# Relation types in the slots of the gathered rows, eight blocks of rows held, and the last four node blocks as two groups of two

## The reference

```
x = x + GRU(red, h)    h = layernorm(x), red[n] = sum over edges to n of h[src] + relvectors[type]
x = x + FFN0(layernorm(x))       shared MLP and 4 experts, top 2
x = x + out / (deg + 1)          out[n] = sum over edges to n of (layernorm(x) @ W.T + b)[src]
x = x + FFN1(layernorm(x))       8 experts of 256 x 1024 x 256, top 2
```

## Time and profile before

| | us |
|---|---|
| median of 3 runs | 3529.81 (3520.11 to 3531.26) |
| the profiled execution | 3538.93 |
| its span | 3537.4 |
| PE busy | 2454.6 (69%) |
| POOL busy | 1839.2 (52%) |
| DVE busy | 1507.1 (43%) |
| ACT busy | 767.8 (22%) |

### The profile page before, as it was taken

How to read it: one execution, slowest core, us unless ns; L and a number is a source line. 1 busy time by engine, 2 the same in 40 slices (tenths; PEclk the granted TensorE clock), 3 DMA queues, 4 the chain that set the end, 5 groups by cost and what they waited for, 6 DMA issues and landing times. The chain is left out here.

```text
span 3537.4 us, 56704 instructions
## 1 busy us (share of the span) xinstructions
PE 2454.6 (69%) x14176; PEld 1894.3 (54%) x14177; DVE 1507.1 (43%) x3886; ACT 767.8 (22%) x1370; POOL 1839.2 (52%) x2044
## 2 busy tenths in 40 slices
PE   1288888888877666546577766654444799999991
PEld 1265555555555453324355544333222699999991
DVE  5544444444453342313466454442311544555545
ACT  1222222222222111002111100000000345444450
POOL 0243334444555566770777777777775344444440
PEclk7578788788777776557677776666555899999996
DMA  5321122122222223330433333333332222211116
GB/s 136 97 62 50 52 59 71 58 69 70 82 76 79 82 83 95 102 101 9 116 109 109 102 113 107 107 107 101 110 104 83 80 66 67 67 58 62 54 44 227
DMA packets 157788, 302.92 MB, mean 86 GB/s; under 512 B 47333, under 2 KB 91784, under 8 KB 157720
## 3 DMA queue, kind: packets, MB, share of 16 engines
q0 software_dynamic: 85984, 234.74, 22.9%
q1 hardware_dynamic: 40876, 36.11, 3.4%
q10 hardware_dynamic: 30860, 31.40, 2.7%
HBM read 261.73 MB, written 40.39 MB: 85 GB/s over the span
## 5 line engine op out<-in xcount | busy, mean ns | idle before, releaser
L733 POOL DMA_INDIRECT rows<-table,srcT x1568 | 1536.5, 980 | 942.8 <-issue 465.7
L793 PE MATMUL bank<-rows,onehot 128*128 x3904 | 794.2, 349 | 673.7 <-POOLq L726 553.7
L793 PEld LDWEIGHTS bank<-rows,onehot 128*128 x3904 | 417.8, 113 | 908.6 <-issue 780.2
L759 DVE SCALAR_TENSOR_TENSOR onehot<-iota_row,tbase,dstT 128x512 f16 x488 | 367.2, 754 | 639.5 <-PE bank L793 225.9
L1733 PE MATMUL bank<-xe_high,W_high 128*128 128x256 f32 x864 | 252.7, 292 | 30.2 <-DVE xe_low L1811 30.0
L1783 ACT ACTIVATE hid<-bank,b 128x256 f32<-128x256 f32 x432 | 181.8, 472 | 346.6 <-PE bank L1735 346.4
L1734 PE MATMUL bank<-xe_low,W_high 128*128 128x256 f32 x864 | 250.7, 290 | 0.0
L1735 PE MATMUL bank<-xe_high,W_low 128*128 128x256 f32 x864 | 250.3, 290 | 0.0
L1819 DVE TENSOR_TENSOR hid_low<-hid,hid_high 128x512 fp32r<-128x512 f32 x216 | 149.7, 693 | 235.9 <-ACT hid_high L1787 235.9
L1733 PE MATMUL bank<-W_high,hid_high 128*128 128x256 f32 x864 | 248.3, 287 | 0.0
L1735 PE MATMUL bank<-W_high,hid_low 128*128 128x256 f32 x864 | 243.8, 282 | 0.0
(11 more groups left out here) (340 smaller groups left out, 3744.1 us busy)
## 6 DMA issues: line engine op xcount, KB each, us to landing
rows<-table,srcT POOLq DMA_INDIRECT x1568, 2.8
W<-in_L_ffn_W_dram SPq DMA_DIRECT2D x14, 1024.0 KB, 7.4
y<-results ACTq DMA_DIRECT2D x12, 1024.0 KB, 10.0
x_res<-in_x_dram SPq DMA_DIRECT2D x1, 6144.0 KB, 44.1
table<-part ACTq DMA_DIRECT2D x12, 512.0 KB, 3.2
normal<-xn ACTq DMA_DIRECT2D x12, 512.0 KB, 3.4
out_dram<-x_res SPq DMA_DIRECT2D x12, 512.0 KB
table<-part SPq DMA_DIRECT2D x6, 512.0 KB, 2.9
```

The source lines that it names most:

```text
L733: nc.gpsimd.indirect_dma_start(out=rows[:, k % (M * U), :], out_offset=None, in_=q.table, in_offset=bass.IndirectOffsetOnAxis(srcT[:, k:k ...
L759: last = nc.vector.scalar_tensor_tensor(onehot[:, ds(slot, U), :], iota_row[:, :].unsqueeze(1).to_broadcast([P, U, P]), base, dstT[:, ds(k ...
L793: last = nc.tensor.matmul(sums, hot, ring_rows[:, ds(row0 + (s * PARTS + part_) * D, D)], start=False, stop=False, skip_group_check=True)
```

## The change

- The ring `rows` of layer 0 has a pitch of 544 numbers: 512 gathered ones and two slots of 16 for types. DVE writes the type one-hot of a chunk into the first slot (columns 512 to 527) if this is the block's first use, else into the second, which nothing reads. `typehot` goes; the second matmul of a chunk takes 272 columns, low half and types together, and the third one goes. `typeT` becomes f16.
- `M` = 8: both layers' rings of rows hold eight blocks instead of four. The landing semaphores stay four (`LANDED`). `PASS` is rounded up to a multiple of 8 (208 in place of 200).
- The groups are 1, eleven of 4, and two of 2 tiles (`SIZES`). For the last two, which stand unrolled behind the loop, a window follows steps 0 and 2 only. So step 3 of the second last group follows W48, and only two tiles' steps follow that.
- `ctT` lies in `work[0:16, 0, :]`.

```diff
@@ -33,17 +33,22 @@
 GROUPS = NT // GW
+SIZES = [1] + [GW] * (GROUPS - 1) + [GW // 2] * 2
+LAST = len(SIZES) - 1
 W = GW * P
...
 U = 4
-M = 4
+M = 8
 MH = 8
+LANDED = 4
 BLOCKS = CHUNKS // U
-PASS = BLOCKS + M
+PASS = -(-(BLOCKS + M) // M) * M
 SPAN = 1024
...
 PARTS = 2
+ROW = PARTS * D
+PITCH = ROW + 2 * RELS
 SCALE = 2048.0
@@ -64,7 +69,7 @@
 def program(nc, a, out):
-    assert NT == GROUPS * GW + 1 and EP * EJ * P >= NE and BLOCKS % M == 0 and PASS % M == 0
+    assert NT == GROUPS * GW + 1 and EP * EJ * P >= NE and BLOCKS % LANDED == 0 and M == MH and PASS % M == 0
@@ -109,7 +114,7 @@
         dstT = sb("dstT", [P, KCOLS], F32, graph)
-        typeT = sb("typeT", [P, KCOLS], F32, graph)
+        typeT = sb("typeT", [P, KCOLS], F16, graph)
         srcT = sb("srcT", [P, CHUNKS], I32, graph)
@@ -162,16 +167,20 @@
+        def size(g):
+            return SIZES[g] if isinstance(g, int) else GW
         def first_tile(g):
-            return NT - 1 - g * GW if isinstance(g, int) else g * -GW + (NT - 1)
+            return NT - first_window(g) - size(g) if isinstance(g, int) else g * -GW + (NT - 1)
...
-            return 0 if isinstance(g, int) and g == 0 else GW - 1 - i
+            return size(g) - 1 - i
         def first_window(g):
-            return 0 if isinstance(g, int) and g == 0 else g * GW - (GW - 1)
+            return sum(SIZES[:g]) if isinstance(g, int) else g * GW - (GW - 1)
@@ -216,13 +225,12 @@
-            return (sb(f"rows{n}", [P, M * U, PARTS * D], F16, where),
+            return (sb(f"rows{n}", [P, M * U, (PITCH, ROW)[n]], F16, where),
                     sb(f"onehot{n}", [P, MH * U, P], F16, where), sb(f"spare{n}", [P, 1], F32, where),
...
         rows, onehot, spare, stats, mean_var, stdev, rstd = layer_buffers(0, layer0)
-        typehot = sb("typehot", [P, MH * U, RELS], F16, layer0)
         h4 = sb("h4", [P, GW, D], F32, layer0)
@@ -697,7 +705,8 @@
                 self.table, self.with_types = table, with_types
-                self.landed = [sem(f"{name}_rows_landed{m}") for m in range(M)]
+                self.pitch = PITCH if with_types else ROW
+                self.landed = [sem(f"{name}_rows_landed{m}") for m in range(LANDED)]
                 self.rows_ready = sem(name + "_rows_ready")
@@ -722,7 +731,8 @@
                 def ready(i, blocks):
-                    pool.wait_ge(q.landed[i % M], p * (BLOCKS // M * 16 * U) + (i // M + 1) * (16 * U))
+                    pool.wait_ge(q.landed[i % LANDED],
+                                 p * (BLOCKS // LANDED * 16 * U) + (i // LANDED + 1) * (16 * U))
                     pool.sem_inc(q.rows_ready, blocks)
@@ -731,8 +741,8 @@
                         nc.gpsimd.indirect_dma_start(
-                            out=rows[:, k % (M * U), :], out_offset=None, in_=q.table,
-                            in_offset=bass.IndirectOffsetOnAxis(srcT[:, k:k + 1], axis=0)).then_inc(q.landed[i % M], 16)
+                            out=rows[:, k % (M * U), 0:ROW], out_offset=None, in_=q.table,
+                            in_offset=bass.IndirectOffsetOnAxis(srcT[:, k:k + 1], axis=0)).then_inc(q.landed[i % LANDED], 16)
                     if i > 0:
@@ -747,9 +757,12 @@
         def dve_onehots_of(dve, q, t, j0, j1):
-            before = dve.snap(window_first(dve, t) + t)
+            opening = window_first(dve, t)
+            before = dve.snap(opening + t)
             first = dve.value_load(windows[0:1, ds(t + 2 * NT, 1)], min_val=0, max_val=PASS)
             base = tbase[:, ds(t, 1)]
+            if q.with_types:
+                types = rows[:, :, :].rearrange("p s (c r) -> p (s c) r", r=RELS)
@@ -760,8 +773,15 @@
                 if q.with_types:
+                    first_use = 1 if j0 > 0 or isinstance(t, int) and t == 0 else (j + (MH - 1)) // MH
+                    at = dve.snap(ring(dve, dve.snap(opening + j), M) * (PITCH // RELS) + (PITCH // RELS - 1) - first_use)
+                    at = narrow(at, 0, ((M - 1) * U + 1) * (PITCH // RELS) - 1)
                     last = nc.vector.tensor_tensor(
-                        typehot[:, ds(slot, U), :], iota_row[:, 0:RELS].unsqueeze(1).to_broadcast([P, U, RELS]),
+                        types[:, ds(at, U, PITCH // RELS), :],
+                        iota_row[:, 0:RELS].unsqueeze(1).to_broadcast([P, U, RELS]),
                         typeT[:, ds(k, U)].unsqueeze(2).to_broadcast([P, U, RELS]), ALU.is_equal)
@@ -773,8 +793,7 @@
             blocks = pe.value_load(windows[0:1, ds(t + NT, 1)], min_val=1, max_val=PASS + 1)
-            ring_rows, hots, types = (ring_[:, :, :].rearrange("p s d -> p (s d)") for ring_ in (rows, onehot, typehot))
-            sums, counts = acc[:, 0:D], acc[:, D:D + RELS]
+            ring_rows, hots = (ring_[:, :, :].rearrange("p s d -> p (s d)") for ring_ in (rows, onehot))
             width = D + RELS if q.with_types else D
@@ -782,21 +801,17 @@
                 slot, hot_slot = ring(pe, m, M), ring(pe, n, MH)
-                row0 = narrow(pe.snap(slot * (PARTS * D)), 0, (M - 1) * U * PARTS * D)
+                row0 = narrow(pe.snap(slot * q.pitch), 0, (M - 1) * U * q.pitch)
                 hot0 = narrow(pe.snap(hot_slot * P), 0, (MH - 1) * U * P)
-                type0 = narrow(pe.snap(hot_slot * RELS), 0, (MH - 1) * U * RELS) if q.with_types else None
                 pe.wait_ge(q.hot, n + 1)
...
                     hot = hots[:, ds(hot0 + s * P, P)]
-                    for part_ in range(PARTS):
-                        last = nc.tensor.matmul(sums, hot, ring_rows[:, ds(row0 + (s * PARTS + part_) * D, D)],
-                                                start=False, stop=False, skip_group_check=True)
-                    if q.with_types:
-                        last = nc.tensor.matmul(counts, hot, types[:, ds(type0 + s * RELS, RELS)],
+                    for at, cols in ((0, D), (D, width)):
+                        last = nc.tensor.matmul(acc[:, 0:cols], hot, ring_rows[:, ds(row0 + (s * q.pitch + at), cols)],
                                                 start=False, stop=False, skip_group_check=True)
                 last.then_inc(q.used, 1)
-            nc.tensor.matmul(sums[:, 0:RELS], zlhs, zrhs[:, 0:RELS], start=False, stop=True,
+            nc.tensor.matmul(acc[:, 0:RELS], zlhs, zrhs[:, 0:RELS], start=False, stop=True,
                              skip_group_check=True).then_inc(q.done, 1)
@@ -851,7 +866,7 @@
         red4 = sb("red4", [P, GW, D + RELS], F32, layer0)
-        ctT = sb("ctT", [RELS, W], F32, layer0)
+        ctT = work[0:RELS, 0, :]
         split_parts = sb("split_parts", [P, 8, W], FR, layer0)
@@ -1137,8 +1152,8 @@
         def dve_d2(dve, chain, g, w):
-            if not (isinstance(g, int) and g == GROUPS):
-                normalised(dve, g + 1, GW)
+            if not (isinstance(g, int) and g == LAST):
+                normalised(dve, g + 1, size(g + 1))
             dve.wait_ge(S["back_ps"], g + 1)
@@ -1220,17 +1235,24 @@
                     steps[GW](0, 1)
-            with eng.Fori(3, GROUPS + 1) as g:
+            with eng.Fori(3, LAST - 1) as g:
                 for i in range(GW):
...
                         steps[GW](g - 2, GW)
+            for g in (LAST - 1, LAST):
+                for i in range(GW):
+                    steps[i](g - 1, size(g - 1))
+                    if i % 2 == 0:
+                        gather(g, i // 2)
+                    if i == 0:
+                        steps[GW](g - 2, size(g - 2))
             for i in range(GW):
-                steps[i](GROUPS, GW)
+                steps[i](LAST, size(LAST))
                 if i == 0:
-                    steps[GW](GROUPS - 1, GW)
-            steps[GW](GROUPS, GW)
+                    steps[GW](LAST - 1, size(LAST - 1))
+            steps[GW](LAST, size(LAST))
@@ -1239,11 +1261,8 @@
                 dve_onehots(dve, q, t, True)
-                if i < GW - 1 or isinstance(t, int):
+                if not isinstance(t, int) or t + 1 < NT:
                     dve_onehots(dve, q, t + 1, False)
-                else:
-                    with dve.If(t + 1 < NT):
-                        dve_onehots(dve, q, narrow(t + 1, 0, NT - 1), False)
                 if evacuate:
@@ -1267,7 +1286,7 @@
                           [lambda g, w, f=f: f(act, g, w) for f in (act_d1, act_d2, act_d3, act_d4, act_d5)], act)
-                act.wait_ge(S["table2_out"], 16 * (GROUPS + 2))
+                act.wait_ge(S["table2_out"], 16 * (LAST + 2))
@@ -1409,7 +1428,7 @@
         def pe_e3(pe, g, w):
-            first, last_ = isinstance(g, int) and g == 0, isinstance(g, int) and g == GROUPS
+            first, last_ = isinstance(g, int) and g == 0, isinstance(g, int) and g == LAST
             for k in range(2 * w):
@@ -1537,7 +1556,7 @@
                                               nothing, nothing, nothing], act)
-                act.wait_ge(R["xn_out"], 16 * (GROUPS + 1))
+                act.wait_ge(R["xn_out"], 16 * (LAST + 1))
...
             def _(dve):
```

## The result

The changed kernel takes 3481.9 us (median of 4, 3473.6 to 3484.3) against 3529.0 for the kernel before on the same chip: 0.9861, 95% interval 0.9847 to 0.9875, 47 us less by the medians and 49 by the ratio. The forecast was 3359, range 3325 to 3425: right in sign, and 123 us too fast.

A forecast was written before the change was run, and what follows sets the result against it. Early windows were taken as bound by the chain PE-ACT-DVE, late ones by POOL stalls and PE's row waits, layer 1's gather by POOL. Terms -50, -42, -30, -24, -21, -4 sum to -171: 3359 us, range 3325 to 3425.

The forecast's parts named there:

- Eight held rows: Both layers' gathers: POOL stalls and PE's row waits shrink; -50 up to W44, -30 in W45 to W48, -20.6 in layer 1.
- Tails: After each layer's gather: two-tile steps shorten the work behind the last window; -24 in layer 0, -4 in layer 1.
- hide behind POOL at 258 us: W45 to W48: POOL sets 258 us in place of 288.6, and the moved dense steps fit behind it.
- Two matmuls instead of three: Layer 0's gather before W45: PE saves 0.56 us a block by less dispatch, on some 85 block uses, 48 us.
- The dispatch rival: Layer 0's gather: dropping the third matmul saves only 0.07 us a block, -5; total 3427, chance 0.13.
- DVE's slot index: DVE's one-hots in layer 0: +0.3 us each, on the path only behind pe_d2, 12 us, half covered.
- the second rival: Layer 0's one-hots: the index at +0.75 us each costs 30 behind pe_d2 and 10 elsewhere; 3403, chance 0.10.
- the forecast's 1211 and 1470: Layer 0's gather: expected signs, W45 starting near 1211 and W48 ending near 1470.

The follow-up runs named there:

- m8: The kernel before with only the rings of eight held blocks and `ctT` inside `work`, types and groups as before: ratio 0.9723.
- m8_groups: The change without the types in the slots (`typehot`, its third matmul and DVE's old index kept), with eight held rows and groups of two: 0.9659.
- m8g_pe: `m8_groups` with two matmuls a chunk, the second reading 16 constant columns, DVE's one-hots as before: W48's end at 1479.2; total time can't be compared.
- after_pad100: The change with 100 semaphore increments on DVE ahead of layer 0's work on the node blocks: 0.9739.
- m8g_own: `m8_groups` with type one-hots placed by the slot index on DVE, in their own buffer, PE keeping its third matmul: 0.9846.
- peel_nolate: The change without the branch for windows over 8 blocks, each window's first block written out without type one-hot, shorter index for the others: 0.9476, 3347.7 us.
- after_pad: The change with 40 semaphore increments on DVE ahead of its loop over groups in layer 0: 0.9838.
- before_pad65: The kernel before with 65 semaphore increments on DVE ahead of layer 0's work on the node blocks: 1.0026 when run again on another chip.

## Why the prediction was wrong

**Eight held rows** (-50, -30 and -20.6): between the traces `m8` gained 67 us up to W45, 34 in W45 to W48 and 14 in layer 1; by its ratio it is 98 us in all (the profiled execution of before lay 9 us above its median, that of `m8` 4 below). Right in mechanism, and in size as a sum; the parts are off by up to 17 us.

**Tails** (-24 and -4): -28.5 and -11 in the trace of after. Right in kind; the second is beyond its bound of -10. Of these 40 us, `m8_groups` keeps 23 against `m8`: the moved steps make W45 to W48 longer by 15 us (269.1 against 254.4). The forecast had them hide behind POOL at 258 us, so this overlap was missed by some 11 us; with two matmuls (`m8g_pe`) it is still 265.9.

**Two matmuls instead of three** (-48): -33 in `m8g_pe`, by W48's end. Right in mechanism, a third too large. The dispatch rival (-5; 0.07 us by 85 uses would be -6) falls: with it W45 would have stayed near 1240, and it starts at 1213.

**DVE's slot index (+6).** This is the step that failed: "I take +0.3 us each, of which the three or four behind pe_d2 lie on the path, 11 groups x 3.6 x 0.3 = 12, half of it covered". It was wrong in all its factors. The size is +0.49 us (0.90 to 1.39), and 0.74 in one window of four. The place is not only behind pe_d2: the one-hots stand ahead of `split_parts` (pe_d1), of `h` (pe_d3) and of the gates' product (pe_d4) as well, and with PE's row waits gone nothing covers them. And nothing was half covered: from `m8g_pe` to `after_pad100` W48's end moves from 1479.2 to 1548.4, 69 us. 244 blocks at 0.49 are 120 us, so more than half of it reaches the time. Of these 69 us, some 23 are PE running at a lower granted clock. This was the second rival, "DVE's slot index becomes the bound", given 0.10 and 3403; even it took only the windows behind pe_d2 and 10 us besides. Its price per one-hot, 0.75, was too high, its reach too short. `m8g_own` adds the point that the sum missed: once DVE sets the pace, the -33 of PE is gone as well: with the index, three matmuls and two take the same time. The terms were added though one cancels the other.

**The place of DVE's code (+43)** was in no step and no rival. That the gap comes with it is shown by padding alone in both kernels. The place costs 43 us in the change, all in layer 0, where the gaps are 22.7 us; in the kernel before 52.9 us of gaps cost 9.

The sum with the measured terms: -120 for `m8_groups` (0.9659), -33, +69 and +43 make -41 (each from one kernel to the next, in the order `m8_groups`, `m8g_pe`, `after_pad100`, the change); measured is -49. The 8 us left are within the intervals. Without gap and index `m8g_pe` met the forecast's 1211 and 1470 to 2 and 9 us. That is partly luck: up to W45 the held rows gave 17 us more than forecast, and two matmuls some 20 less (W45 from 1242.7 to 1213.3, 29 us, for 48).

The way of reasoning that misled: DVE was 42% busy in 799:1280, and that was set against the rival. Busy time doesn't count registers, and an engine that is idle for most of the time was on the path at several of the steps, because every engine keeps one written order.

What stays open: why the boundaries lie some 134 listed instructions apart, and what makes the 0.25 us more in one inner loop. That it goes with the place is shown by `after_pad100`; no run shows its mechanism.

## What to carry to other kernels

Price a computed address on the engine that computes it, per instruction, and against the period of the instruction pair, not its duration; in a kernel where all engines keep one order, ask at each step what stands behind the new work, and don't add a saving on one engine to a cost on another that takes over the path. After any edit of a loop's code look at the back edge in the timeline, and at the packets of the instruction queue: a gap there is paid by place, and some idle instructions ahead, or a shorter body, can remove it. Whether it costs anything depends on what the other engines have to do meanwhile: nothing in layer 1, and in layer 0 of the change more than its length. A block of work that two neighbours share should be done once, outside the loop: together with a shorter index it gave more (75 us) than the whole change (49).

## What the runs showed of the hardware

- A slot index computed on DVE for each pair of operations of 0.75 and 0.22 us (a modulo, a multiplication, a subtraction and the test for first use) brings its period from 0.90 to 1.39 us. Without that test it is 1.15 (`peel_nolate`).
- DVE's loop over the groups (some 310 to 360 instructions) has a gap at its back edge or none, depending on 45 to 65 instructions of place. From the branch to the next instruction it is 2.7 to 3.3 us, against 0.2 to 0.3 without a gap (the 16 turns of `after_pad`: layer 0 with, layer 1 without). Each gap goes with five packets more in the instruction queue, one of them inside the gap.
- A branch that isn't taken cost 21 us in the kernel (0.9659 to 0.9600). It stands in 36 windows of layer 0 and as many of layer 1; by the traces all of it falls in layer 0.
- Where PE waited longer, its own work was slower too: 872 us for the same matmuls at a mean granted clock of 0.82, against 849 at 0.85 (`after_pad100` and `m8g_pe`).
- One chip took 18% longer for the three kernels that ran there. PE's waits in its gather loop were of the loop itself and less of rows, 108.2 us of them against 553.7 (`before_pad65`; the kernel before has 70.9 us, 108 times, 0.8 at most in the row below on its own chip). Its cause stays open:

```profile
PE bank L793 <- issue: 603.8, 512, 8.1
```
